# Attention: product of context and inverted sums moved behind six maxima of the next unit, biases folded into the residual, maxima turned one step sooner

## The reference

```python
x = x + 0.5 * ffn(layernorm(x))
x = x + attn(layernorm(x))      # B=8, S=512, D=512, 16 heads of 32
x = x + 0.5 * ffn(layernorm(x))

def attn(x):
    q, k, v = split(x @ Wqkv.T + b_qkv)
    scores = (q @ k.T) / sqrt(32) + alibi_bias, masked causally
    ctx = softmax(scores) @ v
    return ctx @ Wout.T + b_out
```

## Time and profile before

| | us |
|---|---|
| median of 3 runs | 2989.32 (2983.1 to 2996.19) |
| the profiled execution, its own time | 2996.35 |
| its span, first to last instruction | 2994.7 |

### The profile page before, as it was taken

One profiled execution on the slowest core, in us unless ns is written; L12 is line 12 of the kernel. 1 busy time (PEld: TensorE's weight loads), 2 busy tenths in 40 slices (PEclk: granted clock), 3 DMA queues, 4 the chain that ended last, 5 costly groups with the idle time before them and its releaser, 6 DMA issues. The chain is left out here.

```text
span 2994.7 us, 67665 instructions
## 1 busy us (share of the span) xinstructions
PE 2560.6 (86%) x13156; PEld 1880.3 (63%) x13157; DVE 1419.1 (47%) x3702; ACT 1492.8 (50%) x3700; POOL 1095.5 (37%) x913
## 2 busy tenths in 40 slices
PE   0219999999999368999989899898599999999994
PEld 0117888888888344555555555554278888888883
DVE  8774554555543324443453544434245555555431
ACT  0216666666655314353443534343256666666652
POOL 3434555655555200101011000101245556555552
PEclk9999999999999779988999998998799999999997
DMA  5436877878854423222322323233167777788545
GB/s 154 135 121 161 186 180 181 184 187 190 189 96 56 100 57 76 83 66 84 93 78 85 86 81 76 70 79 86 67 168 176 187 187 173 186 193 197 97 54 144
DMA packets 184823, 377.86 MB, mean 126 GB/s; under 512 B 37629, under 2 KB 88701, under 8 KB 184482
## 3 DMA queue, kind: packets, MB, share of 16 engines
q0 software_dynamic: 76416, 168.58, 29.0%
q1 hardware_dynamic: 97440, 198.30, 22.5%
q10 hardware_dynamic: 10882, 10.14, 1.2%
HBM read 236.63 MB, written 126.88 MB: 121 GB/s over the span
## 5 line engine op out<-in xcount | busy, mean ns | idle before, releaser
L504 POOL DMA_INDIRECT x_rows<-f_ob,f_it x320 | 510.0, 1594 | 578.9 <-ACT f_ob L651 234.9
L554 PE MATMUL f_psg<-f_wh,f_xh 128*128 x1280 | 535.5, 418 | 4.4 <-DVE f_idle L715 2.2
L554 PE MATMUL f_psg<-f_wh,f_xl 128*128 x1280 | 505.2, 395 | 0.0
L554 PE MATMUL f_psg<-f_wl,f_xh 128*128 x1280 | 502.6, 393 | 0.0
L496 POOL DMA_INDIRECT f_xg<-xn_rows,f_it x320 | 353.4, 1104 | 112.3 <-issue 92.3
L1330 DVE CUSTOM_DVE_ANT_0 a_psa<-a_psa,cst 128x384 f32<-128x384 f32 (+3 forms) x512 | 250.5, 501 | 205.2 <-PE a_psa L1106 192.8
L1233 ACT ACTIVATE a_pt<-a_psb 128x256 f32<-128x256 f32 (+3 forms) x512 | 212.5, 435 | 265.0 <-PE a_psb L1159 260.3
L1025 POOL CAST a_cth<-a_ct 128x512 fp32r<-128x512 f32 x32 | 19.5, 610 | 815.9 <-DVE a_ct L1350 725.7
L651 ACT ACTIVATE f_ob<-f_pso,f_wcol 128x512 f32<-128x512 f32 x320 | 220.5, 689 | 192.7 <-PE f_pso L568 192.4
L722 DVE TENSOR_TENSOR f_xl<-f_psx,f_xh 128x512 fp32r<-128x512 f32 x320 | 221.3, 692 | 138.3 <-ACT f_xh L632 138.2
L554 PEld LDWEIGHTS f_psg<-f_wh,f_xl 128*128 128x128 f32 x1280 | 241.9, 189 | 57.6
(11 more groups left out here) (189 smaller groups left out, 4401.7 us busy)
## 6 DMA issues: line engine op xcount, KB each, us to landing
f_wraw<-w_in SPq DMA_DIRECT2D x128, 768.0 KB, 6.7
a_stq<-a_qk SPq DMA_DIRECT2D x128, 144.0 KB
a_stk<-a_qk SPq DMA_DIRECT2D x128, 144.0 KB
r_xt<-x_in SPq DMA_DIRECT2D x32, 256.0 KB, 4.4
xn_rows<-r_xo SPq DMA_DIRECT2D x32, 256.0 KB, 2.9
a_xt<-x_rows SPq DMA_DIRECT2D x8, 1024.0 KB, 5.5
a_x<-x_rows SPq DMA_DIRECT2D x8, 1024.0 KB, 5.4
x_rows<-a_x POOLq DMA_DIRECT2D x8, 1024.0 KB, 5.0
```

The source lines that it names most:

```text
L504: g.indirect_dma_start(x_d, bass.IndirectOffsetOnAxis(it[:, n:n + 1], 0), ob[:, n % OB, :], None, compute_op=ALU.add).then_inc(s_sca[n % O ...
L554: mm = pe.matmul(psg[:, j, :], x[:, j, k, :], w[:, cols], start=(k == 0 and n == 0), stop=(k == DC - 1 and n == 2))
```

## The change

1. DVE's order at a unit's end. `normalise(u - 1)` stands behind maximum i = 5 of the next unit. At the end of g = 3, where values and output follow, it stays where it was.
2. ACT's `high` for q goes from behind exponential n = 1 to behind n = 3, DVE's `low` for q from i = 4 to i = 8.
3. The maxima are turned at n = 14, ahead of the last `psb` product, except in the units with g = 1, where tiles of the next batch are turned over too and it stays at n = 15.
4. Biases. Since the probabilities of a row sum to one, the bias of the values adds the same row to every context. The opening now makes b_v @ Wout.T + b_out once, in 13 products into `psx`, and keeps it, the same row in all partitions, in `bout`. POOL adds it to the residual in unit g = 3 (four additions of 128x512), and the 64 bias products of the tiles are gone. In the opening the bias rows are split before the weights, and their load is a precondition for the first weight piece on ACT; b_v is loaded a second way, one element to a partition and chunk.

```diff
@@ opening @@
+            bv, bvb = xn[:, 0, 0:DC], [xtl[:, :, n * P:(n + 1) * P] for n in range(2)]
+            psx = c1.enter_context(nc.psum_tensor("a_psx", [P, D], F32))
...
-                    sp.wait_ge(s_rows, 80)
+                    sp.wait_ge(s_rows, 64)
+
+                @block.tensor
+                def _(pe):
+                    pe.wait_ge(s_c, 2)
+                    pe.wait_ge(s_br, 16)
+                    pe.wait_ge(s_wl, len(pieces))
+                    pe.wait_ge(s_bvl, 1)
+                    pe.matmul(psx[:, :], ones2, brow, start=True, stop=False)
+                    for k in range(DC):
+                        for p, q in ((0, 0), (0, 1), (1, 0)):
+                            mm = pe.matmul(psx[:, :], bvb[p][:, k, :], wout[q][:, k, :], start=False,
+                                           stop=(k == DC - 1 and p == 1))
+                    mm.then_inc(s_bo, 1)
...
+                    a.dma_start(bv, d["bvo"][0:1, 0, :].rearrange("a (k p) -> (a p) k", p=P),
+                                allow_slow_non_contiguous=True).then_inc(s_in, 16)
+                    a.wait_ge(s_in, 64)
+                    a.activation(biases[32:33, 0, :], rows, ACT.Copy).then_inc(s_bh, 1)
+                    a.activation(bvb[0], bv.unsqueeze(2).to_broadcast([P, DC, P]), ACT.Copy).then_inc(s_bvh, 1)
                     for i, (k, n) in enumerate(pieces):
...
-                    a.activation(biases[32:33, :, :], rows, ACT.Copy).then_inc(s_bh, 1)
+                    a.wait_ge(s_bo, 1)
+                    a.activation(bout[:, :], psx[:, :], ACT.Copy)
@@ GpSimd @@
+                def add_bias(b):
+                    g.wait_ge(s_xr, b * 16 + 16)
+                    g.sem_inc(s_spare_g, 1)
+                    for t in range(TB):
+                        g.tensor_tensor(x2[:, t, :], x2[:, t, :], bout[:, :], ALU.add).then_inc(s_xb, 1)
...
+                        if g4 == NG - 1:
+                            add_bias(b)
                     split_context(b, NG - 1)
@@ TensorE @@
-                def biased(out, which, lhs, rhs):
-
-                    pe.matmul(out, ones2, brow[:, which, :], start=True, stop=False)
-                    return product(out, lhs, rhs, range(DC), begun=True)
...
-                            if a_on and n == 15:
+                            if a_on and n == (15 if x_on else 14):
                                 turn_maxima(bk, u + 1, g, (g + 1) % 2)
@@ ScalarE @@
-                            if n in (1, 7) and not (last and g >= 2):
+                            if n in (3, 7) and not (last and g >= 2):
                                 high(bk, u + 2, g, (g + 2) % NG, n // 7)
@@ VectorE @@
+                            if i == 5 and g:
+                                normalise(u - 1)
-                            if i in (4, 11) and not (last and g >= 2):
+                            if i in (8, 11) and not (last and g >= 2):
                                 low(bk, u + 2, g, (g + 2) % NG, i // 11)
...
-                        normalise(u)
+                        if g == NG - 1:
+                            normalise(u)
```

More of the change, by code:

```diff
@@ L855, in attend @@
         biases = sb("biases", [64 + HG * TB, 2, S], F32R)
-        bias_r, brow = biases[0:H, :, :], biases[32:34, :, :]
+        bias_r, brow = biases[0:H, :, :], biases[32:34, 0, :]
+        bout = sb("bout", [P, D])
         xt = sb("xt", [P, TB, D])
@@ L876, in attend @@
             bias, ones_r = xt[0:H, 0, :], qk3[0:H, 0, 0, :]
-            rows, rows_l, ones = xt[32:33, 1:3, :], xth[32:33, 0:2, :], xt[32:34, 0, 0:P]
+            rows, rows_l, ones = xt[32:33, 1, :], xth[32:33, 0, :], xt[32:34, 0, 0:P]
+            bv, bvb = xn[:, 0, 0:DC], [xtl[:, :, n * P:(n + 1) * P] for n in range(2)]
+            psx = c1.enter_context(nc.psum_tensor("a_psx", [P, D], F32))
             sem1 = lambda n: c1.enter_context(nc.semaphore(f"a_{n}"))
             s_wh, s_wl, s_rows, s_in, s_c, s_bh, s_bl = (sem1(n) for n in ("wh", "wl", "rows", "in", "c", "bh", "bl"))
+            s_br, s_bvh, s_bvl, s_bo = (sem1(n) for n in ("br", "bvh", "bvl", "bo"))
             s_ld = [sem1(f"ld{r}") for r in range(RY)]
@@ L897, in _ @@
                     sp.wait_ge(s_bl, 1)
-                    sp.dma_start(raw(biases[33:34, :, :]), raw(rows_l)).then_inc(s_rows, 16)
-                    sp.wait_ge(s_rows, 80)
+                    sp.dma_start(raw(biases[33:34, 0, :]), raw(rows_l)).then_inc(s_br, 16)
+                    sp.wait_ge(s_rows, 64)
[11 more added lines that the diff above has]
+                    mm.then_inc(s_bo, 1)
                 @block.scalar
                 def _(a):
-                    for dst, src in ((bqk[:, :], d["bqk"]), (rows, d["bvo"]),
-                                     (bias, d["bias"])):
+                    for dst, src in ((bqk[:, :], d["bqk"]), (rows, d["bvo"][0, 1:2, :]), (bias, d["bias"])):
                         a.dma_start(dst, src).then_inc(s_in, 16)
+                    a.dma_start(bv, d["bvo"][0:1, 0, :].rearrange("a (k p) -> (a p) k", p=P),
[3 more added lines that the diff above has]
+                    a.activation(bvb[0], bv.unsqueeze(2).to_broadcast([P, DC, P]), ACT.Copy).then_inc(s_bvh, 1)
                     for i, (k, n) in enumerate(pieces):
@@ L909, in _ @@
                                      scale=1.0 if n else SCALE).then_inc(s_wh, 1)
-                    a.wait_ge(s_in, 48)
                     a.activation(bqk[:, 0:DC], bqk[:, 0:DC], ACT.Copy, scale=SCALE)
-                    a.activation(biases[32:33, :, :], rows, ACT.Copy).then_inc(s_bh, 1)
+                    a.wait_ge(s_bo, 1)
+                    a.activation(bout[:, :], psx[:, :], ACT.Copy)
                 @block.vector
                 def _(v):
+                    v.wait_ge(s_bh, 1)
+                    v.tensor_tensor(rows_l, rows, biases[32:33, 0, :].bitcast(F32), ALU.subtract).then_inc(s_bl, 1)
+                    v.wait_ge(s_bvh, 1)
+                    v.tensor_tensor(bvb[1], bv.unsqueeze(2).to_broadcast([P, DC, P]), bvb[0].bitcast(F32),
+                                    ALU.subtract).then_inc(s_bvl, 1)
                     for i, (k, n) in enumerate(pieces):
@@ L1068, in take, with product @@
                     return psw[:, bk.bank(name, i), :]
-                def product(out, lhs, rhs, chunks, begun=False):
+                def product(out, lhs, rhs, chunks):
                     for k in chunks:
                         for n, (p, q) in enumerate(((0, 0), (0, 1), (1, 0))):
-                            mm = pe.matmul(out, lhs[p](k), rhs[q](k), start=(k == 0 and n == 0 and not begun),
+                            mm = pe.matmul(out, lhs[p](k), rhs[q](k), start=(k == 0 and n == 0),
                                            stop=(k == DC - 1 and n == 2))
                     return mm
-                def biased(out, which, lhs, rhs):
-                    pe.matmul(out, ones2, brow[:, which, :], start=True, stop=False)
-                    return product(out, lhs, rhs, range(DC), begun=True)
                 def turn_x(bk, nb, t):
@@ L1116, in values @@
                         out = take(bk, "v", t)
-                        biased(out, 0, [lambda k, x=x: x[:, k, t * P:(t + 1) * P] for x in (xth, xtl)],
-                               [lambda k, w=w: w[:, k, 2 * D:3 * D] for w in wqkv]).then_inc(s_w, 1)
+                        product(out, [lambda k, x=x: x[:, k, t * P:(t + 1) * P] for x in (xth, xtl)],
+                                [lambda k, w=w: w[:, k, 2 * D:3 * D] for w in wqkv], range(DC)).then_inc(s_w, 1)
                 def output(bk, b):
@@ L1123, in output @@
                         out = take(bk, "o", t)
-                        biased(out, 1, [lambda k, x=x: x[:, k, t * P:(t + 1) * P] for x in (cth, ctl)],
-                               [lambda k, w=w: w[:, k, :] for w in wout]).then_inc(s_w, 1)
+                        product(out, [lambda k, x=x: x[:, k, t * P:(t + 1) * P] for x in (cth, ctl)],
+                                [lambda k, w=w: w[:, k, :] for w in wout], range(DC)).then_inc(s_w, 1)
                 def context(u, g, kt, part):
```

9 lines of the change are left out of this document (4 added, 5 removed).

## The result

| | before | after |
|---|---|---|
| median, both run in turn on one chip | 2991.83 (2983.1 to 2996.19) | 2906.98 (2902.78 to 2913.26) |
| span of the profiled execution | 2994.7 | 2901.1 |
| granted clock, mean | 0.943 | 0.954 |

The ratio is 0.9722, 95% interval 0.9691 to 0.9752. The forecast was 2907. The total is right, but several of the terms that made it up are not, and the profile after shows so at once. Medians and ratios further down leave out two runs that took far longer than the others of the same kernel, one of 3544 us and one of 11087. First the stretches of after: the opening, the main loop in two parts, then one unit each of g = 1, 2 and 3 (columns as in the earlier trace rows).

What follows compares the result with a forecast made beforehand. PE was taken as the bound, through its idle waits and 154 us at 1.2 GHz. Terms -31 - 5 - 5 - 20 - 27 + 6 = -82 us gave 2907 us on the median, range 2872 to 2948.

Steps and rivals of the forecast that it cites:

- Step 3: Later `high` for q on ACT: part of PE's waits for exponentials goes, -5 us, bounds 0 and -10.
- Step 1: Product into `ct` behind six maxima: 23 waits of PE for DVE at unit borders go, -31 us, bounds 0 and -36.
- Step 2: Maxima turned sooner at unit ends: PE waits less for the second row's DMA, -5 us, bounds 0 and -10.
- Step 4: PE's clock in units behind borders: stays up at two thirds of them, -20 us, bounds 0 and -53.
- what is late next: Behind the moved product, PE's first product into psc at n = 5 waits for `normalise`; costed at nothing.
- Rival E: Slower: PE's product into psc waits for `normalise` at n = 5; 3020 us at 4 us a border; chance 0.05.
- Step 5: Values and output tiles: 64 bias products go at 0.43 us each, -27 us, bounds -20 and -30.
- Step 6: The opening: 13 products and a later start on the weights lengthen it, +6 us, bounds +2 and +13.
- Rival B: Main loop: the waits go but the clock stays as low, -62 us, 2927 us; chance 0.20.
- rival C: Borders: SP's 20 copies land later, so ACT's `high` holds n = 6; about 2960 us; chance 0.08.
- D: No gain: copies stall at n = 6 and the clock falls in most units; 2980 to 2995 us; chance 0.05.
- a new wait of PE of more than 1 us at n = 5 or 6: Main loop units: if PE gets such a wait, over 1 us a unit, the prediction calls itself wrong.

Runs made afterwards that it cites:

- only_high: The kernel before with only ACT's `high` for q moved behind n = 3 and DVE's `low` for q behind i = 8: 2949.18 us, ratio 0.9846.
- undo_norm: The changed kernel with the product into `ct` back at the end of every unit: 2888.15 us, ratio 0.9647.
- norm_pool: The kernel before with the product behind six maxima and POOL's inverse deviations ahead of its context split, `high` unmoved: 3010.94 us, ratio 1.0063.
- pool_first: The changed kernel, but in g = 1 POOL computes the next batch's inverse deviations ahead of splitting the context: 2861.61 us, ratio 0.9552.
- open_late: pool_first with the opening's bias splits moved behind weight pieces and PE's product for bout made chunk by chunk: 2856.0 us, ratio 0.9531.
- max_early: pool_first with the first four maxima of the next batch taken inside DVE's output work: 2860.93 us, ratio 0.9559.
- pairs_all: open_late with all five engines' batch loops written out two batches to a body for the first four batches: 2857.26 us, ratio 0.953.

## Why the prediction was right in sum and wrong in its terms

By the runs, going from before: `high` and `low` later 46 us, product and sooner turn on top of it 20.7 (2949.18 to 2928.5), biases 21.5. That is 88, against 85 measured directly; the difference is within what before moves by. That the sum met 2907 is luck. Step 3 gave 41 us more than put down, and steps 1, 2 and 4 together, put at 56, gave some 35 less: two misses of opposite sign (the clock has a share in both). Only biases and opening, put at 21, came out as summed. What a part is worth depends on the others, too: the product with the turn gave 20.7 us on top of only_high, and the product cost 19 on top of turn and biases.

- **Step 1, -31.** Wrong as made: on top of the others it cost 19. The waits at the borders did go, at less than the price that the prediction gave them (with POOL's order turned, 26.5 us with its share of the clock; the sooner turn had already shortened two of the three waits of a batch). The step that failed is "what is late next": it followed the product to PE's `psc`, where no wait came, and not to POOL, whose split also waits for `ct`, with the inverse deviations behind it in its queue. Rival E asked the right question of one reader of the product only.
- **Step 2, -5.** Not measurable with part 1 in place, though its row fell as said, from 18.7 to 9.3. The prediction held that PE gets no more by it than it waited for the row. It also shortens the wait of step 1, which the sum then counts whole (undo_norm against only_high).
- **Step 3, -5.** Mis-sized: alone it gave 46. The prediction worked out a floor of 20.9 us for a unit after and concluded "the copies therefore don't bind". It didn't work out the floor of before. The probabilities' products of one unit of before, n = 4, n = 6 and n = 11:

```profile
1443.91 0.34 PE L1157 MATMUL a_psb<-a_stq,a_stk 100*128 100x384 f32 x1
...
1446.71 0.33 PE L1157 MATMUL a_psb<-a_stq,a_stk 100*128 100x384 f32 x1
...
1451.21 0.28 PE L1157 MATMUL a_psb<-a_stq,a_stk 100*128 100x256 f32 x1
```

  The copies start behind n = 11, at 1451.60, and have landed at 1465.99, where ACT's wait for them ends: 14.4 us. `high` takes 1.1 and the exponential 0.5. With `high` behind n = 1 that lets PE have n = 4, and from n = 4 to the next start of the copies 7.7 us pass (1443.91 to 1451.60): 23.7 us. With `high` behind n = 3 it is n = 6 and 4.9 us: 20.9. Both are estimates from these rows, and they hold for the way from one `high` to the next over the border of g = 2 and 3, not for a unit as the table counts it. That way took 24.1 to 27.3 us before and takes 21.6 to 22.8 after. So before stood close to its floor. What the runs show is two limits of nearly the same height in a g = 2 unit: with the copies' limit lowered and PE's wait at the border left, the best still takes 23.2 us (only_high); with the wait gone and the copies' limit left, 25.3 (norm_pool); with both gone 19.8 (after; 0.7 of it by the sooner turn). Each hid the other, and the prediction saw one.
- **Step 4, -20.** The main loop ran 154 us at 1.2 GHz; after, it is (1 - 0.96) x 2 x 364 + (1 - 0.94) x 2 x 470 = 86, and in pool_first (1 - 0.97) x 2 x 834 = 50. By the prediction's own price of 0.28 us each, the 68 us that went are worth 19, an estimate that no run measures by itself. So the size was about right, but not the places. It went from the borders and stayed at g = 1, where it follows the new stall. The Trainium skill, TensorE: Matmul & The Clock Gate, "HAM oscillation — how this bites in real kernels", had no fall at gaps as short as those borders'. The rows go on speaking against it: undo_norm, with a wait of 1.4 to 1.6 us at the border into g = 2, has 3.9 us at the lower clock in that unit; pool_first, with none over 0.6 there, has none. But units with such a wait that stayed at full clock exist too (1.63 us in a g = 2 unit of before, 1.34 in a g = 1 unit of only_high), so a wait of that size doesn't decide it alone.
- **Step 5, -27.** Too small, for the pitch of a tile; the stretches give 36. The output's additions in after:

```profile
1464.11 0.69 DVE L1385 TENSOR_TENSOR a_x<-a_psw,a_x 128x512 f32<-128x512 f32 x1 [2.06 <-PE a_psw L1106]
1466.86 0.69 DVE L1385 TENSOR_TENSOR a_x<-a_psw,a_x 128x512 f32<-128x512 f32 x1 [1.45 <-PE a_psw L1106]
```

  The pitch is 2.75 us where 3.0 was foretold; before it was 3.38 (1501.79 to 1505.17). A bias product cost 0.63 us of a tile, not the 0.43 between its start and the next. In before, the products around one start 0.33, 0.43 and 0.34 us apart (1484.32, 1484.65, 1485.08, 1485.42), the others of the tile 0.23. So the intervals on both sides of it are longer, and the prediction took one of the three.
- **Step 6, +6.** It was +7.6, and for the reasons given: ACT starts on the weights 7.0 us behind their first load instead of 3.0, with four pieces lying ready, because it waits for the load of b_v; and from the last low part to the main block's first load 7.5 us pass instead of 4.0, with the products between.

Two counts in the sum are off, by a microsecond or so: of the seven stalls behind outputs the last is 2.26 us and not 3.5, and there are eight borders out of g = 2, not seven.

Rival B (waits go, the clock stays) is refuted, rival C's stall came only without part 2, and D and E didn't come. The forecast's own sign of being wrong, a new wait of PE of more than 1 us at n = 5 or 6, did show, in seven of the 32 units: the 3.86 us stand behind the `psb` product of n = 5, one instruction ahead of the first product into `psc`. But PE waits there for a maximum that POOL's queue holds up, not for `normalise`, which had ended at 1385.55.

## What to carry to other kernels

When an instruction is moved later, follow every engine that waits for it, and on each of them name what stands *behind* the waiting instruction in its queue; here a 1.3-us helper on an engine that is 39% busy cost 45 us. Before calling a resource harmless, work out its floor for the kernel as it is, not only for the kernel to come: two limits of the same height hide each other. Two edits in one chain can be worth nothing alone and much together (product and later `high`), or the reverse (product and sooner turn), so time them in both orders.

## What the runs showed of the hardware

DVE stands still at the turn of its loop of batches, for 1.1 to 1.4 us in before and open_late and 3.7 in max_early, with no semaphore to wait for that the profile shows. Written out for two batches it doesn't, but then 1.3-us waits appear 4 us behind the turns that are left, and in pairs_all one such halt of DVE is 3.14 us:

```profile
1685.06 0.30 DVE L1372 CUSTOM_DVE_ANT_0 a_psa<-a_psa,cst 128x128 f32<-128x128 f32 x1 [3.14 <-issue]
```

That it goes with the turn is shown; what DVE waits for there, and why the halt differs in length, no run here shows. Open is also what would gain the 2.2 us of DVE's order together with the halt.
